# Gated products of a mixture-of-experts FFN on GpSimd: two units in one instruction

## The reference

```python
x = x + conv_ref(_ln_c(x), Wq, Wk, Wv, Wb, Wo)      # DeltaNet: 12 heads of 16, sequential over tokens
t = _to_tokens(x)
t = t + ffn_ref(_ln_t(t), router_w, w_gate, ...)    # 8 experts of 192, top 2, and a shared FFN of 768

# in conv_ref, per head:  u_t = beta_t * (v_t - S^T k_t);  S = S + k_t u_t^T;  o_t = S^T q_t
# in ffn_ref:
g = silu(einsum('bsd,edh->bseh', x, w_gate))
u = einsum('bsd,edh->bseh', x, w_up)
expert_out = einsum('bseh,ehd->bsed', g * u, w_down)
shared = silu(x @ ws_gate) * (x @ ws_up) @ ws_down
return alpha * shared + (1.0 - alpha) * routed
```

## Time and profile before

| | |
|---|---|
| device time, median of 3 runs | 483.62 us (483.32 to 485.1) |
| the profiled execution | 484.68 us, its span 482.9 us |
| granted TensorE clock in it | 1.0 of full speed |
| VectorE busy | 415.3 us, 86% of the span, 2258 instructions |
| TensorE matmuls busy | 416.3 us, 86%, 2400 instructions |
| GpSimd busy | 410.8 us, 85%, 525 instructions |
| ScalarE busy | 347.4 us, 72%, 1003 instructions |

### The profile page before, as it was taken

One profiled execution on the slowest core, in us unless ns is written; L12 is line 12 of the kernel. 1 busy time (PEld: TensorE's weight loads), 2 busy tenths in 40 slices (PEclk: granted clock), 3 DMA queues, 4 the chain that ended last, 5 costly groups with the idle time before them and its releaser, 6 DMA issues.

```text
span 482.9 us, 10362 instructions
## 1 busy us (share of the span) xinstructions
PE 416.3 (86%) x2400; PEld 384.6 (80%) x2400; DVE 415.3 (86%) x2258; ACT 347.4 (72%) x1003; POOL 410.8 (85%) x525
## 2 busy tenths in 40 slices
PE   1445265999999999999999999999999989899996
PEld 0323144898998999999999999999999979799895
DVE  4259899999999999999999999999999999996200
ACT  3699466587878687787878696969696847475862
POOL 4479798999999999999999999999999999986340
PEclk9999999999999999999999999999999999999999
DMA  6658372633233323323232233323232332300301
GB/s 163 164 131 176 92 194 76 124 88 117 78 83 80 88 65 96 76 87 87 71 87 83 87 87 83 93 80 92 72 99 71 84 90 76 94 5 1 115 2 16
DMA packets 43437, 42.91 MB, mean 89 GB/s; under 512 B 20144, under 2 KB 35184, under 8 KB 43376
## 3 DMA queue, kind: packets, MB, share of 16 engines
q1 hardware_dynamic: 42768, 42.05, 32.8%
q10 hardware_dynamic: 608, 0.21, 0.2%
HBM read 35.95 MB, written 6.29 MB: 87 GB/s over the span
## 4 chain that ended last, share of the span: by engine, by line
DVE 58%; PE 15%; POOL 9%; issue 8%; SPq 5%; DMA 3%; ACT 2%; POOLq 0%; ACTq 0%; DVEq 0%
DVE Pr L1363 13%; DVE bank L1367 13%; DVE u L1365 12%; DVE SH L1371 10%; PE bank L463 3%; POOL PQ L940 3%; POOL PQ L933 2%; POOL hid L978 2%; PE bank L436 1%; DMA k_scratch<-khl 1%; SPq L278 1%; PE bank L448 1%; PE bank L440 1%; PE bank L439 1%; PE bank L438 1%
## 5 line engine op out<-in xcount | busy, mean ns | idle before, releaser
L978 POOL TENSOR_TENSOR hid<-sg,ug 128x192 f32<-128x192 f32 x192 | 112.7, 606 | 22.0 <-ACT ug L707 18.8
L933 POOL TENSOR_TENSOR PQ<-SH,QB 128x768 f32<-128x768 f32 x62 | 112.6, 1838 | 0.7 <-DVE SH L1371 0.7
L706 ACT ACTIVATE sg<-bank 128x192 f32<-128x192 f32 x192 | 64.4, 336 | 61.1 <-PE bank L440 48.2
L940 POOL TENSOR_TENSOR PQ<-PQ 128x768 f32<-128x768 f32 (+2 forms) x93 | 102.9, 1106 | 6.1
L463 PE MATMUL bank<-Wd,hidT 128*128 128x192 f32 x576 | 106.6, 326 | 0.0
L1367 DVE TENSOR_TENSOR bank<-bank,u 128x96 f32<-128x96 f32 (+1 forms) x467 | 104.7, 266 | 0.6
L1363 DVE TENSOR_TENSOR Pr<-SH,bank 128x96 f32<-128x96 f32 (+1 forms) x437 | 101.3, 266 | 3.3 <-PE bank L403 1.3
L1365 DVE TENSOR_REDUCE u<-Pr 128x6 f32<-128x102 f32 (+1 forms) x437 | 102.6, 269 | 0.4
L1371 DVE TENSOR_TENSOR SH<-SH,bank 128x96 f32<-128x96 f32 (+1 forms) x467 | 102.2, 257 | 0.3
L463 PEld LDWEIGHTS bank<-Wd,hidT 128*128 128x128 f32 x576 | 94.5, 190 | 0.0
L436 PE MATMUL bank<-Whi,hiT 128*128 128x384 f32 (+1 forms) x192 | 73.1, 381 | 1.1 <-DVE loT L1134 1.1
(11 more groups left out here) (141 smaller groups left out, 815.9 us busy)
## 6 DMA issues: line engine op xcount, KB each, us to landing
QB<-q_scratch SPq DMA_DIRECT2D x64, 384.0 KB
k_scratch<-khl SPq DMA_DIRECT2D x64, 48.0 KB, 1.7
KR<-k_scratch SPq DMA_DIRECT2D x32, 96.0 KB, 2.4
q_scratch<-qn SPq DMA_DIRECT2D x64, 24.0 KB, 1.6
Wd<-in_L_ffn_w_down_dram SPq DMA_DIRECT2D x4, 288.0 KB, 7.6
out_dram<-xT SPq DMA_DIRECT2D x1, 896.0 KB, 4.1
Wlo_unsplit<-in_L_ffn_w_gate_dram SPq DMA_DIRECT2D x2, 384.0 KB, 4.6
Wlo_unsplit<-in_L_ffn_w_up_dram SPq DMA_DIRECT2D x2, 384.0 KB, 5.7
```

The source lines that it names most:

```text
L933: tt(PQ[:, at * BR * HP:(at + n) * BR * HP].rearrange("p (i b h) d -> p i b (h d)", i=n, b=BR), SH[:, lo:lo + n].rearrange("p i b h d -> p ...
L940: chained(tt(PQ[:, :, 0:w], PQ[:, :, 0:w], PQ[:, :, w:2 * w], ALU.add))
L978: tt(hid[:, r * H:(r + 1) * H], sg[:, m % RING], ug[:, m % RING], ALU.mult).then_inc(s_hid, 1)
```

## The change

`hidden` is called for m = 0, 2, 4, 6, 8 and 10 only and multiplies units m and m + 1 in one instruction of 384 columns; it waits for both to be copied and adds two to `s_hid`. Its place in GpSimd's list: products 6 and 7 stand where product 7 stood, behind `rsqrt`; 8 and 9 where 8 stood; 10 and 11 where product 11 stood, behind `A_kn`; 0 and 1 where product 1' stood, behind `A_vn`; 2, 3 and 4, 5 behind it. No other engine's code is changed.

```diff
             def hidden(q, p, m):
-                pool.wait_ge(s_ug, q * UN + (m + 1))
+                pool.wait_ge(s_ug, q * UN + (m + 2))
 
                 if m >= UN // 2 or later(q, 1):
-                    last = ((m - UN // 2) % UN + 1) * H - 1
+                    last = ((m + 1 - UN // 2) % UN + 1) * H - 1
                     g = [lo * P <= last < hi * P for lo, hi in GRP].index(True)
                     pool.wait_ge(s_ht, q * NG + (g + 1 - (0 if m >= UN // 2 else NG)))
-                r = m % (UN // 2)
-                tt(hid[:, r * H:(r + 1) * H], sg[:, m % RING], ug[:, m % RING], ALU.mult).then_inc(s_hid, 1)
+                r, s = m % (UN // 2), m % RING
+                tt(hid[:, r * H:(r + 2) * H].rearrange("p (m h) -> p m h", m=2), sg[:, s:s + 2], ug[:, s:s + 2],
+                   ALU.mult).then_inc(s_hid, 2)
 
             def step(c, par):
...
                 elif c < NC:
                     once(c, 1, weights_1, 8)
                     once(c, 1, weights_1, 9)
-                    at(-2, hidden, 6)
                     if c <= NC:
                         rsqrt(c)
-                    at(-2, hidden, 7)
+                    at(-2, hidden, 6)
                     once(c, 1, weights_1, 10)
                     once(c, 1, weights_1, 11)
                     at(0, reading, 0)
                     at(-2, hidden, 8)
-                    at(-2, hidden, 9)
-                    at(-2, hidden, 10)
                     at(0, summing, 0)
                     at(2, A_kn)
-                    at(-2, hidden, 11)
+                    at(-2, hidden, 10)
                     at(2, A_qn)
-                    at(-1, hidden, 0)
                     at(0, reading, 1)
                     at(0, summing, 1)
                     at(2, A_vn)
-                    at(-1, hidden, 1)
+                    at(-1, hidden, 0)
                     at(-1, hidden, 2)
-                    at(-1, hidden, 3)
                     at(-1, hidden, 4)
-                    at(-1, hidden, 5)
                     at(2, A_klo)
```

## The result

The changed kernel takes 536.99 us (median of 4 runs, 534.96 to 537.56) against 483.51 for the kernel before (483.32 to 485.1). The ratio on record is 1.107, 95% interval 1.104 to 1.110 (the two medians alone give 1.111): slower by 53 us. The prediction had the direction, with 514 us and a range of 507 to 522; the loss is about 1.75 times what it gave.

A forecast was written before the change was run, and what follows sets the result against it. VectorE was taken to bound the middle chunks; two parallel rings of 27.4 and 27.2 us, the longer counting, replace 25.2 a chunk, adding 30.5 us in all with the end: 514 us, range 507 to 522.

The forecast's parts named there:

- What bounds the kernel, and that the savings are worth nothing: VectorE bounds the middle chunks, busy 25.06 of 25.20 us; GpSimd's saved 0.9 a chunk is worth at most 0.14.
- Cost of a pair, 1.00 us: One 384-wide GpSimd product takes 1.00 us, 0.95 from its start to the next one's; a single takes 606 ns.
- The 0.83 weighed beside it: The Trainium skill's rule for a two-input GpSimd instruction of 384 elements: 0.83 us, giving a total near 505.
- Product 10 moved to 11's place, turn 3 at 11.9 after `rsqrt`: Group 3 waits for pair (10, 11), so TensorE's turn 3 comes 11.9 us after `rsqrt` instead of 9.8.
- The ring behind it, 27.2 us: From `rsqrt` through pair (10, 11), turn 3, fill 0 and VectorE's slot 0 to `Fa_stats`, back to `rsqrt`: 27.2 us.
- Product 0 moved, 27.4 us: Unit 4 waits for pair (0, 1), delaying up 6, `Fa_y`, `Fa_stats` and the next `rsqrt`: 27.4 us a chunk, now 25.2.
- They do not add: The two rings run side by side and share the stretch from `rsqrt` to pair 10, so only the longer counts.
- The rival in which the stalls add up: TensorE's two waits do not overlap: 2.1 + 2.2 us a chunk, 56 us in all, 540 us; chance 0.04.
- The sign that I had named for it, chunks near 29: Chunks near 29 us, from `rsqrt` to `rsqrt`, would say that the two waits add.
- The other pairs cost nothing, and what product 6 leaves costs nothing: Pairs (2, 3) and (4, 5) stay covered, else tenths; product 6 behind `rsqrt` only lets the wait there absorb freed time.
- The sum: The chunks' and the end's delays add to +30.5 us on a profiled execution of 484.68: 515.2, median 514.
- the ring through unit 4: From `rsqrt` to product 0 done 21.40, unit 4's copy 0.64, up 6 to `Fa_y` 4.17, `Fa_stats` to `rsqrt` 1.03, handovers 0.15: 27.4 us.

The follow-up runs named there:

- two_six_single: Kernel before with pairs for products (4, 5) and (8, 9) alone, all else as in it; 484.82 us, ratio 1.001.
- ring6_free: Kernel before with pairs (0, 1) behind `A_vn`, (4, 5), (8, 9), and rings of six places for sg and ug instead of four; 485.52 us, 1.003.
- warm_units: Changed kernel with products 10 and 11 single again, plus 20 useless transposes on TensorE right before up 6; 521.05 us, ratio 1.078.
- warm: Changed kernel with 20 useless transposes on TensorE right before turn 3 in chunks 0 to 13; 523.69 us, ratio 1.081.
- zero_single: Changed kernel with products 0 and 1 single again, 0 ahead of reading 1, 1 behind `A_vn`; 535.56 us, ratio 1.103.
- both_single: Changed kernel with products 0, 1, 10 and 11 single again in their old order, the other pairs kept; 495.37 us, ratio 1.022.
- order_only: Kernel before, all products single, but in the changed kernel's order; 525.15 us, ratio 1.084.
- ten_single: Changed kernel with products 10 and 11 single again, 10 behind pair (8, 9), 11 behind `A_kn`; 533.38 us, ratio 1.101.

## Why the prediction was wrong in its size

- **What bounds the kernel, and that the savings are worth nothing.** Right. two_six_single and ring6_free save instructions where nobody waits, and give no time.
- **Cost of a pair, 1.00 us.** Right: 1006 ns. The 0.83 weighed beside it did not hold.
- **Product 10 moved to 11's place, turn 3 at 11.9 after `rsqrt`.** Right, 12.22 (254.65 - 242.43). 0.16 of the excess is the pair (6, 7), which starts 0.82 after `rsqrt` (243.25 - 242.43) where product 7 started 0.66 after it; unit 7, for which both wait, is copied only when `rsqrt` ends.
- **The ring behind it, 27.2 us: the step that failed.** It took TensorE's work behind the wait, down 2 and fill 0, with durations from a trace in which TensorE never stood still for long, and so put the cost of a lower clock at nothing, without a word on it. Behind a wait of 2.99 us TensorE's clock was halved for most of 4.6 us. Fill 0 ended 2.84 after turn 3 began instead of 2.10. VectorE took 270.54 - 257.52 = 13.02 for the 12.04, because TensorE stays late: 0.32 of waiting for a fill (L403), 0.18 for a projection (L376), some 0.1 at `Fa_stats`, and smaller gaps. The ring that really closed runs along TensorE's own order, from turn 3 to the end of `Fa_y`: 12.22 + 15.85 + 1.07 (to `rsqrt`) = 29.14 us. I had said that a late TensorE only reaches up 6 later; I did not add that stretch up as a ring. But adding it up would not have found the loss. In the trace before it is 14.24 us, so the ring comes to 11.92 + 14.24 + 1.03 + 0.10 = 27.3, hardly more than the 27.2. What was missing is the clock, 15.85 for 14.24.
- **Product 0 moved, 27.4 us.** The mechanism is real: it gives 27.9 alone at full clock in warm_units, and it holds up 6 in warm, where its ring is 27.78. But in the changed kernel it is not on the path (zero_single). The forecast took it for the longer ring by 0.2; with the half clock turn 3's is longer by 1.2.
- **"They do not add."** Right, for the reason given. The rival in which the stalls add up gave 540, near the result, by a mechanism that the runs exclude: without unit 4's wait nothing changes. The sign that I had named for it, chunks near 29, did appear (29.07) and would have misled: the half clock gives the same length.
- **The other pairs cost nothing, and what product 6 leaves costs nothing.** True only under the longer rings. Once those are gone they cost 11 us (both_single); undone one at a time they give back 6 and 7. The text had said tenths, and tenths a chunk they are, 25.88 - 25.29 = 0.6; the rest of the 11 us lies outside iterations 2 to 12.
- **The sum.** The profiled executions compare as 537.56 and 515.2, so 22.4 us were missing. Up to iteration 12 they are 389.17 - 372.8 = 16.4, in iterations 13 to 15 another 3.9 (472.82 - 452.5 is 20.3), and in the end 2.1. Of the 1.67 a chunk (29.07 - 27.4) the clock is 1.27, by the difference to warm. The other 0.4 are terms of the ring through unit 4, as warm shows it: product 0 is done 21.62 after `rsqrt` and not 21.40, mostly by the late pair (6, 7); up 6 to the end of `Fa_y` takes 4.28 and not 4.17; the handovers are a little longer.

## What to carry to other kernels

When engines are in step within tenths, price a move by what each of its waiters does next, and close every ring, the waiting engine's own program order among them; two rings may each be enough, and undoing one then shows little. Where a change makes TensorE stand still anew, as for 3 us in each chunk here, price its next few microseconds of work at half clock as well as at full. The test for it is to fill the wait with matmuls that nobody needs. In this kernel, joining two instructions on an engine that was not the bound saved nothing, and where a result was wanted before the later of the two, it cost.

## What was not expected of the hardware

In the chunk shown TensorE's clock was still full while it stood still (1.00 at 250.0 to 254.6, busy for 1.65 of 4.6 us) and fell after the work had come (0.64 in the next 4.6). In the chunk ahead of it the clock fell before the work came, and turn 3 took 1.11 us instead of 0.66:

```profile
225.67 1.11 PE L448 MATMUL bank<-ident,hid 128*128 128x128 f32 x4 [2.97 <-POOL hid L978]
```

```profile
224.20:225.60 1.40, 0.00 (x0) 0.00 (x0) 1.40 (x10) 1.40 (x5) 1.40 (x3) 0.85 0.51 143
```

Between iterations 2 and 12 the clock fell in nine of ten chunks of the changed kernel (waits of 3.0 to 3.2 us), in six of ten of order_only (2.6 to 3.0 us) and in four of ten of ten_single (2.4 to 2.9 us). The length of the wait alone did not decide: the changed kernel's 3.10 us kept the clock, and a 2.44 us wait of ten_single lost it. At the start of a run it differs between executions at no cost: two_six_single has 0.74 over its first 100 us, 1.00 from 100 to 400, and is as fast as the kernel before, whose profiled execution has 1.0 throughout; so the mean clock of a run says little of what it costs.

```profile
0.00:100.00 100.00, 49.01 (x182) 37.44 (x183) 74.58 (x403) 65.62 (x168) 76.33 (x106) 0.74 0.59 141
100.00:400.00 300.00, 290.61 (x1763) 274.84 (x1762) 296.64 (x1644) 230.63 (x694) 283.14 (x335) 1.00 0.30 84
```
